# Recurrence: the bank's starting values written by ScalarE instead of by a product with the identity

## The reference, cut to what matters

```python
def step(S, ins):
    q_t, k_t, v_t, a_t, b_t = ins
    read = jnp.einsum('bhk,bhkv->bhv', k_t, S)
    err = read - v_t
    S = a_t[:, :, None, :] * S - b_t[:, :, None, None] * k_t[..., None] * err[:, :, None, :]
    o_t = jnp.einsum('bhk,bhkv->bhv', q_t, S)
    return (S, o_t)
```

## Time and profile before

| | |
|---|---|
| time, median of 3 runs | 1919.13 us (1919.01 to 1919.22) |
| the profiled execution's own time | 1919.19 us |
| its span | 1917.1 us |
| TensorE busy (matmul) | 1703.5 us, 89%, 15702 instructions |
| TensorE weight loads | 1445.2 us, 75% |
| VectorE busy | 1362.2 us, 71% |
| ScalarE busy | 1000.8 us, 52% |
| GpSimd busy | 619.1 us, 32% |

### The profile page before, as it was taken

The page is one execution under the profiler, slowest core; times in us unless marked ns, Lnnn a source line. Parts: engine busy times, 40 slices in busy tenths (PEclk is TensorE's granted clock), DMA queues, the critical chain, the costliest instruction groups (busy, mean ns, idle before and its releaser), DMA issues. The chain is left out here.

```text
span 1917.1 us, 42317 instructions
## 1 busy us (share of the span) xinstructions
PE 1703.5 (89%) x15702; PEld 1445.2 (75%) x15702; DVE 1362.2 (71%) x3230; ACT 1000.8 (52%) x2618; POOL 619.1 (32%) x975
## 2 busy tenths in 40 slices
PE   4599999899999999999988598999999999998895
PEld 3477778787877778877876365688888888888794
DVE  4688777877788777877775475566666666664777
ACT  2355555555555555565543354556566656652353
POOL 6455345543555335543451122000000000001653
PEclk9799999999999999999988799999999999999898
DMA  6212331323222332323320200990000000003232
GB/s 216 59 51 65 75 86 49 68 59 85 65 56 65 75 87 46 74 67 75 83 50 23 90 1 5 183 14 2 2 2 2 1 2 1 2 2 107 65 93 76
DMA packets 150338, 106.78 MB, mean 56 GB/s; under 512 B 34132, under 2 KB 138648, under 8 KB 149240
## 3 DMA queue, kind: packets, MB, share of 16 engines
q1 hardware_dynamic: 147640, 98.95, 23.7%
q0 software_dynamic: 2496, 5.13, 0.8%
HBM read 86.06 MB, written 17.99 MB: 54 GB/s over the span
## 5 line engine op out<-in xcount | busy, mean ns | idle before, releaser
L593 POOL TENSOR_TENSOR kfull<-kt,pair_rows 128x512 f32<-128x512 f32 x128 | 143.6, 1122 | 517.2 <-ACT kt L381 513.5
L361 PE MATMUL ps<-xT,taps 128*128 128x128 f32 x2048 | 276.8, 278 | 0.1
L853 ACT COPY wt<-ps 32x128 f32<-32x128 f32 x512 | 131.7, 257 | 263.9 <-PE ps L748 256.9
L361 PEld LDWEIGHTS ps<-xT,taps 128*128 128x128 f32 x2048 | 258.7, 196 | 7.6 <-issue 7.2
L1687 DVE TENSOR_REDUCE b_nmax<-ps 128x1 f32<-128x128 f32 (+7 forms) x256 | 180.6, 752 | 72.9 <-PE ps L1524 72.9
L896 DVE TENSOR_TENSOR prod<-ps,mt 128x128 f32<-128x128 f32 x512 | 147.4, 288 | 78.6 <-PE ps L759 62.7
L748 PE MATMUL ps<-ident,w 128*128 128x128 f32 x512 | 162.9, 318 | 34.6 <-ACT wt L853 18.5
L1664 POOL COPY b_spread<-b_inv 128x256 f32<-128x256 f32 x64 | 25.8, 402 | 513.2 <-DVE b_inv L1690 513.2
L899 DVE TENSOR_REDUCE w<-prod 128x32 f32<-128x128 f32 x512 | 146.5, 286 | 17.5
L748 PEld LDWEIGHTS ps<-ident,w 128*128 128x128 f32 x512 | 88.1, 172 | 84.9 <-DVE w L899 73.6
L1616 ACT ACTIVATE b_prob_long<-ps,b_nmax 128x1024 f32<-128x1024 f32 (+3 forms) x128 | 121.4, 953 | 55.7 <-DVE b_nmax L1687 55.7
(11 more groups left out here) (308 smaller groups left out, 3843.2 us busy)
## 6 DMA issues: line engine op xcount, KB each, us to landing
decay<-ends_dram SPq DMA_DIRECT2D x256, 128.0 KB, 5.5
gn<-near_dram SPq DMA_DIRECT2D x32, 384.0 KB, 6.9
slots_dram<-zero SPq DMA_DIRECT2D x1, 9216.0 KB, 59.3
rr<-rates_dram SPq DMA_DIRECT2D x32, 256.0 KB, 4.5
sq<-rstd_dram SPq DMA_DIRECT2D x16, 512.0 KB, 3.6
wtap<-in_taps SPq DMA_DIRECT2D x4, 1024.0 KB, 11.2
f_w<-in_f_w SPq DMA_DIRECT2D x2, 2048.0 KB, 10.4
s_xb<-slots_dram SPq DMA_DIRECT2D x46, 64.5 KB, 1.8
```

Of the source, the lines that this page charges most:

```text
L361: mm = pe.matmul(part, lhsT=taps[:, tap, t * P:(t + 1) * P], rhs=xT[:, :, columns(at_next) - LOOK + tap:columns(at_next) - LOOK + tap + TS ...
L593: nc.gpsimd.tensor_tensor(kfull[:, n % 4, :, :], kt[:, n % 2, :].unsqueeze(1).to_broadcast([P, G, P]), cst["pair_rows"][:, :].unsqueeze(2) ...
L853: nc.scalar.copy(wt[rows, b, :], ps[rows, 2, 0:P]).then_inc(wt_kept[b], 1)
```

## The change

ScalarE takes over the filling of the bank. A new function `preset` writes zeros over the output columns (a copy of a one-element tile `zero`, spread over 128 columns) and then the values into `z`, each raising the new semaphore `z_set`. It has the waits that `start` had for `prepared` and `o_kept`. It is called twice ahead of the loop, and in each half behind `ring(3)` and ahead of `put_back`, for the (chunk, b) whose `start` comes next on TensorE. `start` loses its product with the identity and those two waits, and waits for `z_set` instead. In the stage before, a product of the identity with the zero state into each of the two banks is added, and a memset of `zero` on GpSimd.

```diff
@@ stage before, block.tensor
                 for b in range(B):
+                    pe.matmul(ps[:, b, :], lhsT=cst["ident"][:, :], rhs=state[:, b, :, :].rearrange("p g v -> p (g v)"),
+                              start=True, stop=True, skip_group_check=True)
                     pe.matmul(ps[:, 4 + b, :], lhsT=cst["ident"][:, :], rhs=state[:, b, :, :].rearrange("p g v -> p (g v)"),
                               start=True, stop=True, skip_group_check=True)
...
@@ stage before, block.gpsimd
                 nc.gpsimd.memset(o[:, 1, :, :, :], 0.0)
+                nc.gpsimd.memset(zero[:, :], 0.0)
...
@@ recurrence, block.tensor
                 def start(cc, b):
                     f, c = cc // NC, cc % NC
-                    if c == 0 and f >= 1:
-                        pe.wait_ge(S["prepared"], 2 * f)
-                    if cc >= 1:
-                        pe.wait_ge(o_kept[b], cc)
-                    vdc = vd[:, f % 2, :, b, :].rearrange("p h (c i s) -> p c i h s", c=NC, s=BK)
-                    pe.matmul(z_of(b), lhsT=cst["ident"][:, :], rhs=vdc[:, c], start=True, stop=False,
-                              skip_group_check=True)
+                    pe.wait_ge(z_set[b], 2 * (cc + 1))
                     if cc >= 1:
                         pe.wait_ge(s_ready[b], cc)
...
@@ recurrence, block.scalar
+                def preset(cc, b):
+                    f, c = cc // NC, cc % NC
+                    if c == 0 and f >= 1:
+                        act.wait_ge(S["prepared"], 2 * f)
+                    if cc >= 1:
+                        act.wait_ge(o_kept[b], cc)
+                    values = vd[:, f % 2, :, b, :].rearrange("p h (c i s) -> p c i h s", c=NC, s=BK)
+                    nc.scalar.copy(ps[:, b, P:2 * P], zero[:, 0:1].to_broadcast([P, P])).then_inc(z_set[b], 1)
+                    nc.scalar.copy(z_of(b), values[:, c]).then_inc(z_set[b], 1)
+
+                preset(0, 0)
+                preset(0, 1)
                 for cc, x, f, j in halves:
...
                     ring(2)
                     ring(3)
+                    if cy >= 0 and cy < last_chunk:
+                        preset(cy + 1, y)
                     if cc >= 1:
                         put_back(cc - 1, x)
```

More of the change, by code:

```diff
@@ L258, in delta_attention @@
         rate_rows = sb("rate_rows", [H, N])
+        zero = sb("a_zero", [P, 1])
         rates_dram = nc.dram_tensor("rates_dram", (2, H, N), F32).ap()
@@ L268, in delta_attention @@
         two = lambda n: [sem(f"a_{n}{b}") for b in range(B)]
-        z_ready, w_ready, wt_ready, wt_kept = two("z_ready"), two("w_ready"), two("wt_ready"), two("wt_kept")
+        z_set, z_ready, w_ready, wt_ready, wt_kept = (two(n) for n in ("z_set", "z_ready", "w_ready", "wt_ready", "wt_kept"))
         p_ready, s_ready, s_back, o_ready, o_kept = (two("p_ready"), two("s_ready"), two("s_back"), two("o_ready"),
@@ L274, in delta_attention @@
         every = list(S.values()) + [dve_chain, pool_chain] + decay_in[0] + decay_in[1]
-        for pair in (z_ready, w_ready, wt_ready, wt_kept, p_ready, s_ready, s_back, o_ready, o_kept):
+        for pair in (z_set, z_ready, w_ready, wt_ready, wt_kept, p_ready, s_ready, s_back, o_ready, o_kept):
             every += pair
```

## The result

The changed kernel takes 1982.18 us (median of 4 runs, 1980.05 to 1983.65), the kernel before beside it 1919.18 (4 runs, 1919.01 to 1921.45). The ratio is 1.0325, 95% interval 1.0307 to 1.0342: 3.3% slower. I had forecast 1982.

What follows compares the result with a forecast made beforehand. TensorE's in-order queue, busy 56.19 of 61.20 us a frame, was taken as the bound. Fourteen inner frames at 3.96 us (55.4), first frame 3.2 and last 3.8 gave 62.4 on 1919.2: 1982 us, range 1960 to 2006.

Steps and rivals of the forecast that it cites:

- The place decides: At start, both ScalarE copies queue behind the kt copy, so TensorE's first state matmul begins 0.71 us after kt does.
- The length of the copies: On ScalarE behind kt: 0.20 us from zeros' start to values' start, then 0.29 until the values are in.
- the rival of slower copies: Strided reads of the values add 0.14 us on 112 to 117 starts: 16 us more, 1998 us; chance 0.12.
- Each delay shifts everything behind it: Rule for the recurrence: every delay of a start passes on whole to all later work, 3.96 us a frame.
- 3.96 us a frame: Sum of net delays over the eight starts of a steady frame, growing it from 61.2 to 65.2 us.
- my own sign: If copies read 0.29 us or less and the frame stays under 64 us, passing on every delay is wrong.
- j=0: First of a frame's eight starts, j=0 to j=7; it waited for VectorE's state anyway, so 0 us was forecast.
- The 1.06 at j=3: Fourth start of a frame: 1.06 us late on TensorE, counted as 0.78 because VectorE was held by the mask.
- it pays off: Rival: copies are covered, only the product's removal counts, 0.32 us on 90 starts, 29 us: 1890 us; chance 0.04.
- ScalarE's time: Copies' load on ScalarE: no separate term; pushes on later ScalarE work entered two starts' delays, 0.42 and 0.40 us.
- The identity products: Two products added ahead of the stage run while TensorE waits for convolution weights; 1 us if uncovered.
- The clock falls: Rival: unbroken pause at each frame's first start lowers TensorE's clock, 6 us a frame, 90 more: 2072 us; chance 0.05.

Runs made afterwards that it cites:

- experiment 1: The changed kernel with preset called ahead of ring(3) instead of behind it: 1923.56 us, ratio 1.002 to the kernel before.
- experiment 2: The changed kernel with preset moved one item later, behind put_back: 2034.91 us, ratio 1.0601 to the kernel before.
- experiment 6: The kernel before, no work added, but TensorE waits in start for the kt copy, behind the product: 1940.01 us, ratio 1.0103.
- experiment 9: The kernel before with two wide GpSimd operations (kfull and the preparation of the values) cut short: 1886.70 us, ratio 0.9827.
- experiment 10: The changed kernel with two wide GpSimd operations (kfull and the preparation of the values) cut short: 1975.73 us, ratio 1.0295.
- experiment 3: The kernel before without the product with the identity and nothing in its place, values left out of the computation: 1920.63 us, ratio 1.0007.
- experiment 11: The changed kernel with preset ahead of ring(3) at five starts a frame, the product kept elsewhere, no added identity products: 1924.56 us, ratio 1.0017.
- experiment 4: The kernel before, product kept, with two ScalarE copies added at preset's place into unused rows, nobody waiting for them: 1952.02 us, ratio 1.0162.
- experiment 5: The kernel before, product kept, with only the values' copy added on ScalarE at preset's place, nobody waiting for it: 1938.35 us, ratio 1.0103.
- experiment 7: The kernel before, product kept, two ScalarE copies added into unused rows, and TensorE waiting for them behind its product: 2005.52 us, ratio 1.0454.
- experiment 8: The changed kernel with only the zeros' copy moved ahead of ring(3), the values' copy staying behind kt: 1976.4 us, ratio 1.0299.

## Why the prediction came out right, and where its terms were off

**The place decides: held.** TensorE waits at 112 starts for copies ordered behind `kt`, at `kt` + 0.68. Moving the same instructions one place ahead takes away 59 us, one place back adds 53 (experiments 1 and 2); the bare wait for `kt` costs 21 us with no work added at all (experiment 6).

**The length of the copies: held.** I took 0.20 from the start of the zeros to the start of the values and 0.29 for the values; they read 0.20 and 0.27. The values' reads at a stride cost nothing (the zeros' copy takes 0.28), so the rival of slower copies falls. The Trainium skill (ScalarE: Activation LUTs, "What ACT_TABLE_LOAD costs") gives 293 ns for such a copy and 200 ns from one to the next, estimates from its formula. The trace agrees on the second (0.20) and is 0.16 behind the copy of `kt`, which reads PSUM.

**"Each delay shifts everything behind it": partly wrong.** I summed 3.96 us a frame (the terms add up to 3.95) and it is 3.10; by my own sign (under 64 us with short copies; it is 64.30) this is just on the side where the rule stands, but start by start it doesn't. From j=0: 0, 0.42, 0.79, 0.78, 0.40, 0.37, 0.59, 0.6 were forecast, -0.17, 0.57, 0.63, 1.05, -0.15, 0.52, 0.57, 0.13 measured. j=1, 2, 5 and 6 agree to 0.16. The 1.06 at j=3, which I cut to 0.78 by VectorE's slack, is passed on whole, but the next start takes 0.15 of it back. The large miss is j=7 with j=0, 0.6 against -0.04, and experiments 9 and 10 show whose it is: VectorE's collisions with GpSimd, which the delay ahead of them moves. With them cut the frame grows by 4.27 us, so the sum of 3.96 was too small for the delays alone and too large only with this relief. I had not looked at GpSimd's timeline at all, and the 1.23 us of a 128x128 operation that takes 0.39 without company stood in the trace of before. The Trainium skill (SBUF — State Buffer, "SBUF: two separate sides") says that a VectorE operation with two SBUF inputs and a GpSimd operation that reads SBUF exclude each other on a shared port for the length of the whole instruction, and that the one which starts first gets it. The trace agrees: L502 ends 0.25 us after GpSimd's `kfull`, 0.26 after it in the changed kernel, and in frame 4, where it is the first, it takes 0.39 and `kfull` 1.28.

**The rival "it pays off": wrongly priced.** I put the removal of the product at 0.32 us on 90 starts, 29 us, and took it for worth having if only the copies were covered. Experiments 1, 3 and 11 cover them, or leave them out, and find -0.1, -0.45 and -0.16 us a frame, and nothing in the total. A queue busy for 56.19 of 61.20 us isn't the bound of the frame where VectorE sets three of its eight starts and ScalarE holds it ahead of a fourth. The 35 waits of the earlier trace rows leave out the short ones, under 0.15 us; the earlier trace rows show VectorE's state ahead of j=0, 4 and 5. This didn't enter the forecast, since I compared starts; it is still the error that would have cost most, had the order on ScalarE been the other one.

**ScalarE's time: not a term, and rightly so.** Added alone it costs 19 to 32 us (experiments 4 and 5), wait alone 21 (6), both with the product kept 86 (7). In the changed kernel it seems covered for the most part by the wait, since TensorE comes later to everything that ScalarE delivers behind it: at j=1 the wait of 0.30 us for `wt` is gone from the timeline. At j=4 it isn't covered, and the wait for `wt` is 0.48 us against 0.31:

```profile
560.48 0.41 PE L757 MATMUL ps<-gq,wt 128*128 128x32 f32 x2 [0.48 <-ACT wt L851]
```

No run shows the size of the covered part by itself.

**The identity products: mis-sized.** I took them as covered, and as 1 us if not. TensorE ahead of the first convolution, kernel before and kernel after:

```profile
22.89 3.75 PE L654 MATMUL ps<-state,ident 128*128 128x512 f32 x4 [22.89 <-PEq L192]
```

```profile
22.15 2.05 PE L655 MATMUL ps<-state,ident 128*128 128x512 f32 x2 [22.15 <-PEq L192]
23.99 1.91 PE L657 MATMUL ps<-state,ident 128*128 128x512 f32 x2
25.70 1.92 PE L655 MATMUL ps<-state,ident 128*128 128x512 f32 x2
27.40 1.26 PE L657 MATMUL ps<-state,ident 128*128 128x512 f32 x2
28.50 5.52 PE L362 MATMUL ps<-xT,taps 128*128 128x128 f32 x48
```

The products take 6.35 us up to L362, against 3.54 up to the first convolution at 26.43, 2.8 more. TensorE was waiting for no weights there, and the stage starts 1.9 later. Over the runs with GpSimd's full work it starts at 69.0 to 70.8 us without the two products and at 70.9 to 72.0 with them.

**"The clock falls": in part.** I gave it 0.05 and 90 us. It does fall, not behind j=0 but between j=2 and j=3, in frames 0, 3, 6, 9 and 12, for 1.5 us each, against one fall in the kernel before; and the last frame is 8.2 us longer where I had 3.8, with the granted clock at 0.78 in its windows against 0.86 (47.39 us of TensorE in 58.85) before. The Trainium skill (TensorE: Matmul & The Clock Gate, "A second HAM failure mode: psum-queue depth-cycling") warns of frequent short idles between groups of matmuls; the trace agrees in that new idles of 0.72 to 1.21 us at `start` go with falls in five frames where the kernel before has one. That one, in frame 5, stands behind the only long pause of its j=0 starts:

```profile
377.24 0.69 PE L737 MATMUL ps<-kq,state 128*64 128x64 f32 x16 [1.43 <-DVE state L912]
```

Experiments 4, 5 and 6, where TensorE idles 0.68 us at most just ahead of the matmuls on the state, have no fall in the 14 inner frames. Why five frames and not sixteen stays open: experiments 7 and 8, in which a start begins 0.83 and 0.49 us after `kt` (0.69 in the change), have 8 and 10.

So the total was met because errors cancel: 11.4 us too much in the inner frames, and too little ahead of the stage (1.9), in the first frame (0.9), in the frames with a fall of the clock (6.7 less the 3.2 by which frames of before are longer than its steady one), in the last frame (4.4) and behind it (1.1), 11.8 together. The place, the sign and the delay of 0.7 us a start were read from the trace; that the sum agrees to 0.2 is luck.

## What to carry to other kernels

When work moves from one engine to another, find the instruction ahead of it in the new engine's program order, and what that one waits for. If it waits for the last thing the consumer issues before it needs the result, the move turns into a wait however idle the new engine is (ScalarE was busy for half of the time here); one item further ahead the same copies cost 4 us and not 63. And before pricing what is removed, look for the next point at which another engine sets the start: 41 us out of an engine at 89% were worth nothing, because three starts in eight belonged to VectorE and a fourth stood behind a wait for ScalarE, and the clock took what was left.

## What the runs showed of the hardware

- A 128x128 VectorE operation on two SBUF operands takes 0.38 to 0.40 us without a wide GpSimd operation beside it and 1.23 when it begins 0.06 us behind one of 1.04. Beginning 0.02 us ahead of it, it took 0.39, and GpSimd's took 1.28. Cutting two wide GpSimd operations short made the whole kernel before 1.7% faster, and changed the price of this edit from 63 to 89 us.
- ScalarE's copies of 128 columns take 0.27 to 0.29 us on average, from PSUM to SBUF, from SBUF to PSUM and from SBUF to SBUF. From the start of one from PSUM to SBUF the next begins after 0.16 us if it goes from SBUF to PSUM, and after 0.29 if it goes from SBUF to SBUF (experiment 4, 64 partitions). Between the starts of two that read SBUF it is 0.20 with the same target, and 0.30 from a target in SBUF to one in PSUM.
- The granted clock fell in some frames and not in others of the same work, at a fixed place in the frame, for 1.5 us each; pauses of about 2.2 us (j=0 of experiments 1 and 3), of 1.43 (frame 5 of the kernel before) or some 0.7 to 1.2 us (the changed kernel) stood ahead of the falls; with 0.68 us at most just ahead of the matmuls on the state (experiments 4 to 6) no inner frame had one.
